# TensorE's loops over the blocks of four Chebyshev propagations, written out with constant addresses

## The reference, cut to what matters

```python
def prop(h):
    return jnp.zeros((n, h.shape[1]), h.dtype).at[row].add(w[:, None] * h[col])
Tx0 = x
out = Tx0 @ W[0]
Tx1 = prop(Tx0)
out = out + Tx1 @ W[1]
for k in range(2, K):              # K = 3
    Tx2 = 2.0 * prop(Tx1) - Tx0
    out = out + Tx2 @ W[k]
    Tx0, Tx1 = (Tx1, Tx2)
return out + b
```

## Time and profile before

| what | value |
| --- | --- |
| time, three runs | 2887.59 us median, 2884.13 to 2894.74 |
| span of the profiled execution | 4076.3 us, 62411 instructions |
| TensorE matmuls busy | 1936.6 us, 48%, x16923 |
| VectorE busy | 2238.4 us, 55% |
| ScalarE, GpSimd busy | 1209.9 us, 1592.5 us |
| matmuls of line 1331 | x2500, from 2235.4 to 2749 us of the span |

### The profile page before, as it was taken

The page is one execution under the profiler, slowest core; times in us unless marked ns, Lnnn a source line. Parts: engine busy times, 40 slices in busy tenths (PEclk is TensorE's granted clock), DMA queues, the critical chain, the costliest instruction groups (busy, mean ns, idle before and its releaser), DMA issues. The chain is left out here.

```text
span 4076.3 us, 62411 instructions
## 1 busy us (share of the span) xinstructions
PE 1936.6 (48%) x16923; PEld 1342.4 (33%) x16923; DVE 2238.4 (55%) x4872; ACT 1209.9 (30%) x3818; POOL 1592.5 (39%) x1665
## 2 busy tenths in 40 slices
PE   5835544454444444330223249992211255655377
PEld 4623333333333333220111126661111245545222
DVE  6876766666676776430211013323211399997899
ACT  1154444444444444230001002100000133334744
POOL 0055555555555555456766640006667400000000
PEclk8966666666666666665555569995555598896599
DMA  8611111111111111542222210004443222221000
GB/s 277 249 42 40 40 40 40 40 40 40 40 40 40 40 40 40 172 124 55 59 52 53 52 34 1 0 11 138 136 115 102 61 75 83 74 82 42 0 0 8
DMA packets 399312, 266.91 MB, mean 65 GB/s; under 512 B 321473, under 2 KB 349310, under 8 KB 399090
## 3 DMA queue, kind: packets, MB, share of 16 engines
q1 hardware_dynamic: 306278, 87.81, 10.1%
q10 hardware_dynamic: 41488, 118.96, 8.1%
q0 software_dynamic: 51488, 59.40, 6.0%
HBM read 158.59 MB, written 107.47 MB: 65 GB/s over the span
## 5 line engine op out<-in xcount | busy, mean ns | idle before, releaser
L1229 POOL DMA_INDIRECT sorted_edges<-r_load,r_to x800 | 792.0, 990 | 736.3 <-DMA r_to<-places 439.6
L805 POOL DMA_INDIRECT hsrc<-h,edges x808 | 778.4, 963 | 693.5 <-PE ps L998 460.1
L873 DVE TENSOR_TENSOR prod<-ps,hsrc 125x1024 f32<-125x1024 f32 x200 | 245.0, 1225 | 323.3 <-remote 180.1
L996 PE MATMUL ps<-blank 128*64 128x160 bf16 x101 | 31.5, 312 | 590.2 <-remote 579.3
L1401 PE MATMUL ps<-R,w_work 128*128 128x64 bf16 x3000 | 145.1, 206 | 272.3 <-DVE R L1743 148.2
L1537 ACT ACTIVATE R<-w_work 128x384 bf16<-128x384 f32 (+1 forms) x160 | 85.8, 536 | 617.6 <-DVE w_work L1733 506.5
L1733 DVE TENSOR_TENSOR w_work<-ps,w_work 128x384 f32<-128x384 f32 (+1 forms) x160 | 91.2, 570 | 306.3 <-remote 296.6
L1391 PE MATMUL ps<-R 128*128 128x64 bf16 x3000 | 142.9, 208 | 225.5 <-issue 132.7
L1331 PE MATMUL ps<-R,A 128*128 128x192 bf16 x1250 | 183.0, 267 | 138.8 <-issue 136.0
L864 DVE TENSOR_SCALAR hot<-ramp,small 125x400 bf16<-125x400 int16 x800 | 219.6, 326 | 49.9 <-issue 47.7
L952 ACT ACTIVATE lo<-ramp,edges 125x128 bf16<-125x128 int16 x808 | 246.8, 387 | 0.0
(11 more groups left out here) (414 smaller groups left out, 4419.4 us busy)
## 6 DMA issues: line engine op xcount, KB each, us to landing
w_work<-sorted_edges ACTq DMA_DIRECT2D x42, 1000.0 KB
sorted_edges<-A ACTq DMA_DIRECT2D x25, 1000.0 KB, 7.3
r_load<-in_edge_attr_dram SPq DMA_DIRECT2D x80, 312.5 KB
dstrow<-dst_rows SPq DMA_DIRECT2D x101, 234.4 KB
counts<-A ACTq DMA_DIRECT2D x5, 4000.0 KB, 30.2
A<-counts SPq DMA_DIRECT2D x12, 1600.0 KB
sorted_edges<-A ACTq DMA_DIRECT2D x3, 5000.0 KB, 28.7
hsrc<-h,edges POOLq DMA_INDIRECT x808
```

The costliest lines, as they stand in the source:

```text
L805: g.indirect_dma_start(out=hsrc[:, s, t, :], out_offset=None, in_=S.h0[:, :], in_offset=bass.IndirectOffsetOnAxis(ap=edges.bitcast(I32)[:, ...
L873: v.tensor_tensor(prod[0:TP, :].rearrange("p (t h f) -> p t h f", t=HT, h=H), S.ps[0:TP, hf * 1024:(hf + 1) * 1024].rearrange("p (t h f) - ...
L1229: g.indirect_dma_start(out=S.sorted, out_offset=bass.IndirectOffsetOnAxis(ap=to[:, hf, t:t + 1], axis=0), in_=load[:, hf, t, :], in_offset ...
```

## The change

The loops over i become Python loops, so that every one of the 2500 matmuls stands in TensorE's program with a constant address, by the function `block_at` that was there before (L1155). Only TensorE's stream changes.

```diff
--- before.py
+++ after.py
@@ -1328,7 +1328,7 @@
                     if linear and j == 17:
                         weigh_block(i * UN + (m - 1), (m - 1) % UN)
-                    mm = pe.matmul(S.bank[m][:, 0:SP3 * D], S.A[:, bass.ds(i * (UN * P) + (j * NP + m * P), P)],
+                    mm = pe.matmul(S.bank[m][:, 0:SP3 * D], block_at(j, i * UN + m),
                                    part[:, j * SP3 * D:(j + 1) * SP3 * D], start=(j == 0), stop=(j == NB - 1))
                 mm.then_inc(p["prod"], 1)
@@ -1336,13 +1336,13 @@
-                    with pe.Fori(1, NB // UN) as i:
+                    for i in range(1, NB // UN):
                         for m in range(UN):
                             block_of(k, i, m, True)
                     turn_block(NB - 1, UN - 1)
                     weigh_block(NB - 1, UN - 1)
                 else:
-                    with pe.Fori(0, NB // UN) as i:
+                    for i in range(NB // UN):
                         for m in range(UN):
                             block_of(k, i, m, False)
```

## The result

The changed kernel takes 2874.43 us (median of five, 2869.81 to 2879.58), the kernel before beside it 2887.77 (five, 2884.13 to 2894.74): a ratio of 0.9952, with a 95% interval of 0.9935 to 0.9968. The forecast was 2830. The four propagations became 69.3 us shorter, 11 more than forecast, and 56 of these were lost again later.

What follows compares the result with a forecast made beforehand. It took TensorE's loops to be bound by their instruction stream, one register instruction per matmul. Gains of 29.7 + 13.9 + 14.3 + 0.5 = 58.4 us took 2887.6 to 2829, forecast 2830, own range 2812 to 2850, 8-in-10 range 2795 to 2874.

Steps and rivals of the forecast that it cites:

- The register instruction's price: TensorE's propagation loops: one register instruction per matmul makes the step 0.124 us instead of 0.0825; 98.6 us over all.
- rival B: TensorE's loops: the 0.124 us step comes from recording, so only 5 to 10 us are gained, 2880; chance 0.07.
- Fourth propagation: k=3: TensorE stays last, 84.7 us become 55, including 3.1 for the low clock at its start; gain 29.7.
- First and third: k=0 and 2: VectorE becomes last at 2.75 us a block, 73.2 us each; gains 14.3 and 13.9.
- rival C: First and third propagation: VectorE is faster than 2.75 us a block, up to 29 each, 2800; chance 0.08.
- Second: k=1: the linear step waits for ScalarE, not the matmuls; gain 0.5 us, bounds -2 and 10.
- D: Written-out TensorE code: instruction fetches are not hidden, 15 packets at 5.93 us cost 89 us, 2918; chance 0.05.
- E: First and third propagation: idle TensorE runs at half clock, 4.0 us a block, 26 lost, 2884; chance 0.03.
- All after the fourth propagation waits for its end and moves up with it: Edge stage, VectorE's at 3.5 us a step: it moves up by the propagations' whole gain, 58.4 us.
- rival A: Edge stage: GpSimd's scatters bind it, taking 0 to 58 us of the gain, middle 2860; chance 0.15.
- 1.53 in its rows: Scatter pace in us recorded beside the stage from 1690, 545/356; at it the scatters take 1224 us, late already.
- the books: Sum of four stages' recorded stretching, meant to account for 1188 us between the span 4076 and the time 2888.

Runs made afterwards that it cites:

- f0: The kernel before, unchanged, run again for a trace on a chip where it takes about 2888 us: 2888.84 us, span 2887.1.
- h1: The changed kernel with L1740 and L1743 written as scalar_tensor_tensors of the same values, on a chip of the second kind: 4030.13 us, ratio 0.9868.
- h2: The kernel before with L1740 and L1743 written as scalar_tensor_tensors of the same values, on a chip of the second kind: 4091.13 us, ratio 1.0006.
- e1: The kernel before with 560 of the 800 scatters, on a chip of the second kind: 3743.23 us, ratio 0.9109.
- e2: The changed kernel with 560 of the 800 scatters, on a chip of the second kind: 3675.17 us, ratio 0.8943.
- e0: The kernel before, unchanged, run again for a trace on a chip of the second kind: 4105.19 us.
- g2: The changed kernel with the second chunk of edges loaded into a free tile before SyncE's other loads: 2873.6 us, ratio 0.9945.

## Why the prediction was wrong

**The propagations: right in kind, somewhat small in size.** TensorE of the changed kernel in the first and the fourth, with its wait ahead of the latter, and VectorE's sums in both, answer to the earlier trace rows:

```profile
1504.52 1.78 PE L1331 MATMUL ps<-R,A 128*128 128x192 bf16 x10
...
1741.31 6.87 PE L1331 MATMUL ps<-w_work,A 128*128 128x192 bf16 x52 [13.17 <-DVE w_work L1631]
```

```profile
1552.16 0.35 DVE L1641 TENSOR_REDUCE c_red<-ps 128x64 f32<-128x192 f32 x1
...
1554.66 0.35 DVE L1641 TENSOR_REDUCE c_red<-ps 128x64 f32<-128x192 f32 x1
...
1770.74 0.36 DVE L1641 TENSOR_REDUCE c_red<-ps 128x64 f32<-128x192 f32 x1 [1.14 <-PE ps L1331]
...
1772.80 0.36 DVE L1641 TENSOR_REDUCE c_red<-ps 128x64 f32<-128x192 f32 x1 [1.14 <-PE ps L1331]
```

- The plain step of TensorE is 0.083 us in all four (median of the starts) and 0.124 in f0. The register instruction's price is as forecast, and rival B falls.
- Fourth propagation: forecast 55, measured 54.2, sums 2.06 apart. Gain 30.5 against 29.7. The low clock at its start costs about 2.4 us and not 3.1 (52 matmuls in 6.87 us, where 4.5 would do).
- First and third: VectorE is late last, as said; its block is 2.54 and 2.59 us (medians of the sums' distances) and not 2.75, so they take 68.4 and 68.0 where the forecast had 73.2. That is a piece of rival C. Gain 18.5 and 18.7, against 14.3 and 13.9. The wait on TensorE at their end is 13.0 and 13.2 us, "some 10" in the forecast.
- Second: forecast 0.5, measured 1.6.
- Sum 69.3 against 58.4. D falls (47 fetched packets, 13 more, and no hole), E falls (the clock is 0.90 and 0.94 in the two windows).

**The step that failed** is "All after the fourth propagation waits for its end and moves up with it". It doesn't: the edge layer's end waits for the last scatter, and that was 3.1 us away in f0 (in an ordinary execution perhaps 10). This is rival A, which had 0.15. It was dismissed by one number, "800 scatters at 1.27 are 1016 us". They are 1148 from the first to the last in f0, 1.44 each, and 1140 after; by the prediction's own condition A "cuts in from 1.35 a scatter on". The 132 us between are read off f0: 40 is GpSimd's wait for the second chunk, 6 a slower third one, and 86 the last twenty-one chunks, from the end of the propagations on, 29.5 us each and not 25.4. A pace that was taken from the propagations, where VectorE and GpSimd hardly meet, was laid over a stage where they do. The prediction had even the better number in hand, 1.53 in its rows, and put it aside as stretched. The other side of the race came out nearly right by luck. The last item's load was forecast to be due 1141 us after the scatters begin and was requested at 1154 in f0, but the propagations end at 537 and not at 566, and an item takes 15.0 us and not 13.9.

**The other error lies under it.** It is "I put this stretching down to the recording", with the books that closed on it. The stretch is that of the other kind of chip: the eight kernels that ran there with all their scatters take 4025 to 4105 us, while f0 was recorded too and spans 2887.1. The books closed because one of their four terms was an estimate and one the remainder. Between the earlier trace rows and f0 the terms are 368 us for the attention stage, 364 for the stage from 1690, 153 for the first propagation and 314 for the edge layer, against 338, 340, 153 and 357. What the books were to show is true all the same: from the second propagation's start to the fourth's end it is 273.1 us in both. On that kind of chip 35 of 40 items are done behind the last scatter, so the trace that I read hid the one race that decides the other kind: who is later in the edge layer, VectorE or GpSimd. There about the forecast's 58 us came, 61.0 (h1, h2) and 68.1 (e1, e2), but with the scatters in full by another path than the forecast's, through SyncE's hold of the last 16 chunks.

## What to carry to other kernels

When work beside the path (here 800 DMAs of GpSimd) must be finished when the path ends, its slack is a term of the sum like any other: take its length from start to end, with its first wait and with its pace in each stage, not from the pace in the quietest one. If the span of a profile and the times differ by 40%, first ask for another profile of the same kernel; an explanation that balances is not yet one. And one part of a change, run alone, tells in one run whether the rest is already lost. A slack of a few us that is read off one trace is that execution's; compare the first instructions of both traces before their ends are subtracted.

## What the runs showed of the hardware

- One program, two speeds: 2886 to 2889 us on two chips, 4089 to 4110 on three. On the latter the engines' instructions stand apart while GpSimd issues DMAs, TensorE in e0's first propagation for instance:

```profile
2236.64 0.32 PE L1331 MATMUL ps<-R,A 128*128 128x192 bf16 x1 [1.08 <-issue]
```

  (108 of its 624 steps are over 0.6 us, most of them about 0.7, 1.4 or 2.8; 0.124 otherwise), though the scatters themselves keep their 0.97. What differs between the chips was not found.
- 1875 more written-out matmuls cost 13 instruction packets in the whole program and run at 0.083 us each. The longest step in the fourth propagation is 0.16 us, so there is no hole.
- A load of 1250 pieces of 8 bytes takes 36 us to issue beside 398 GB/s of traffic, most of it ScalarE's writes of the counts (g2, 1338 to 1375), and about 3 without.
- A GpSimd DMA of 0.97 us grew to as much as 1.85 beside VectorE's two-input instructions L1740 and L1743 (the one that begins at 1871.35 of the changed kernel).
